# Ten of every sixteen scan units injected by VectorE, Silu as one activation, sums of exp(q) by TensorE, and modulation columns used where they lie

## The chip, the cores and the metric

The kernel runs on one NeuronCore of a Trainium2 chip. The metric is device time in microseconds (us) from the start to the end of one execution. The core has five engines that run side by side and meet at semaphores: TensorE (PE), VectorE (DVE), ScalarE (ACT), GpSimd (POOL) and SyncE (SP, which here only issues DMAs).

## What is computed

x has 8 sequences of 512 tokens with 256 features, float32. Four conditioned layers follow each other; the condition `c` has 512 numbers for each sequence. Layers 0 and 3 are linear attention, layers 1 and 2 are selective scans (Mamba). Cut to what matters:

```python
# layers 0 and 3 (16 and 8 heads; in layer 0 the product's orientation differs)
xn = layernorm(x) * g + b
q  = softmax(xn @ Wq + bq, over the features of a head)
k  = softmax(xn @ Wk + bk + mask, over the tokens)
v  = (xn @ Wv + bv) * mask
y  = q @ (k.T @ v)                       # per head
scale, shift = split(silu(c) @ W_emb + b_emb)
h  = layernorm(y) * (1 + scale) + shift
x  = x + silu(h) @ W_out + b_out
# layers 1 and 2
shift, scale, gate = split(silu(c) @ W_ada + b_ada)
xz = (layernorm(x) * (1 + scale) + shift) @ W_in     # layer 2: tokens permuted
u, z = split(xz);  u = silu(conv4(u))
dt_r, Bm, Cm = split(u @ W_x);  dt = softplus(dt_r @ W_dt + b)
for t in tokens:                          # 512 channels x 16 states
    h = h * exp(dt[t] * A) + (dt[t] * u[t]) * Bm[t];  y[t] = (h * Cm[t]).sum()
x = x + gate * ((y + u * D) * silu(z)) @ W_out
```

## The kernel before

**Units.** Each scan (one sequence in one of layers 1 and 2, so 16 scans in all) is cut into 64 units: one of 16 states of one of 4 chunks of 128 channels, a tile of 128 channels by 512 tokens. 1024 units follow each other. Of unit g, ACT makes the decay exp(dt * A) (L887, L903), somebody multiplies dt*u with the row B ("injects"), DVE runs the recurrence as one `tensor_tensor_scan` (L1160, L1163), POOL multiplies the state with the row C (`weight`, L673), and PE adds the result into a bank of y (L1463). Some groups of four tiles are first added to others by a DMA that POOL issues (L677).

**Two kinds of unit.** `KINDS` says which kind each of 16 consecutive units has. BESIDE: POOL injects from SBUF into the state tile (L664), and ACT writes the decay into one of three PSUM banks (L887). SPREAD: ACT copies the row B into the PSUM bank (`b_row_in_bank`, L895) and writes the decay to SBUF (L903), and DVE injects in the bank (L1153). The bank for unit g+2 is filled while unit g is due, and ACT may fill it only when the scan of unit g-1 has ended (`past(act, m_scan, g - BANKS + 1)`). POOL injects unit g+3 and weights unit g-2.

**Everything else is woven in.** Beside the units run chains of work, each a Python generator per engine: 16 attentions (`attention`: layernorm, turns, k, q, v, the mixing product `mix`, y, a second layernorm, the activation `hid`, the output), 16 preparations (`before`: norm, in-projection, convolution, step sizes), 16 ends of scans (`after`: gate row, gated output weights, output, in layer 2 the permuting back), and at the very start the set-up (`setup`: products of silu(c) with the conditioning weights `c0` to `c3`, L1202; modulation columns `m0` to `m3`; gate rows). For each kind of chain a table (`ATT_STAGES`, `PREP_STAGES`, `POST_STAGES`, `TAIL_STAGES`, `SETUP_STAGES`) gives the number of steps each stage lasts; `timeline` stretches the chain over a range of units, and `run_batches` writes each engine's instructions in that order. Every engine then works in that fixed order and waits where a semaphore isn't there yet. The names of the stages are also the places in the tables.

**What the change touches.** The attention's activation is made from tanh, which stands with exp in one activation table: ACT writes s*h into SBUF (L796) and tanh(s*h) into the bank (L797), DVE joins them (L1086). The modulation columns of a sequence are copied by POOL from `mod_all` to `mod_att` and `mod_prep` (L618, L640), and `gate_pick` (L654) picks one row of the gates, with which ACT makes `gate_row` (L871) for a PE product that spreads it over the partitions (L1426). DVE sums exp(q) over each head (L1068) and takes the reciprocal (L1069) ahead of the mixing. An ACT_TABLE_LOAD stands in ACT's order wherever the next function isn't in the table that is loaded: silu, softplus and exp are in three different ones.

Of the kernel before, what the change touches and what calls it, by code (L numbers as in the profile page):

```python
# [5 lines left out]
P = 128  # L6
# [17 lines left out]
SLOTS = 4  # L24
# [39 lines left out]
MOD_PICK = 8 * DC + 2 * TT  # L64
MODS = MOD_PICK + 1
# [14 lines left out]
def by_name(names, durations):  # L80
# [4 lines left out]
    "first": (3, 19, 20, 20, 31, 13, 4, 6, 28, 4, 62, 1, 1, 2, 9, 13, 10, 15, 0, 2, 11, 15, 37, 4, 14, 6, 0, 2, 30,  # L85
              16, 10, 1, 18, 17, 29, 26, 34, 15, 65, 18, 9, 1, 11, 0, 10, 3, 12, 0, 20, 7, 4, 14),
    "second": (2, 1, 3, 2, 0, 4, 0, 3, 3, 4, 4, 2, 3, 3, 3, 0, 0, 4, 0, 2, 5, 14, 1, 22, 2, 0, 16, 3, 1, 0, 2, 0, 6,
# [9 lines left out]
    "last": (8, 7, 10, 2, 26, 4, 13, 17, 8, 24, 13, 58, 8, 11, 1, 12, 8, 4, 27, 33, 3, 6, 46, 2, 11, 1, 34, 2, 16, 11,  # L97
             12, 12, 5, 20, 5, 6, 6, 5, 60, 0, 20, 8, 12, 15, 5, 6, 22, 17, 4, 1, 3, 4),
})
PREP_STAGES = by_name(PREP_NAMES, {  # L100
    "first": (5, 9, 3, 1, 2, 3, 0, 4, 5, 3, 0, 4, 7, 4, 0, 1, 4, 5, 9, 1, 6, 9, 4, 9),
# [4 lines left out]
})  # L106
POST_STAGES = by_name(POST_NAMES, {
# [4 lines left out]
})  # L112
TAIL_STAGES = by_name(TAIL_NAMES, {
    0: (3, 14, 7),
    1: (0, 32, 4),
    2: (14, 7, 5),
    3: (34, 17, 9),
})
SETUP_STAGES = dict(zip(SETUP_NAMES, (0, 1, 1, 0, 15, 38, 1, 22, 3, 24, 3, 10), strict=True))
# [209 lines left out]
def bass_cond_seq(nc, x, out, mask_cols, keep_cols, mask_rows0, mask_rows3, order, const_pack, att_packs, ssm_packs,  # L329
# [4 lines left out]
    with ctx:  # L334
# [29 lines left out]
        def cw(name):  # L364
# [4 lines left out]
        ones_row8 = cw("ones")[on_gates, :]  # L369
# [11 lines left out]
        mod_att = sb("mod_att", [P, 2 * DC + TT])  # L381
        mod_prep = sb("mod_prep", [P, 2 * DC])
        gate_pick = sb("gate_pick", [P, 1])
# [14 lines left out]
        gate_row = sb("gate_row", [P, D])[on_gates, :]  # L398
# [65 lines left out]
        o_pick, o_row = sem("gate_picked"), sem("gate_row")  # L464

        def past(eng, sem_, count):

# [1088 lines left out]
```

## Time and profile before

| | |
|---|---|
| median of 3 runs | 2323.63 us (2316.66 to 2324.0) |
| profiled execution | 2320.92 us; its span 2318.9 us |
| before the first unit (to about 137 us) | set-up, first preparation, first attention |
| the units (about 137 to 2235 us) | 2098 us for 1024 units |
| behind them | end of the last scan, the last two attentions |
| POOL busy | 2000.3 us (86%) |
| DVE busy | 1980.6 us (85%) |
| PE busy | 1931.7 us (83%) |
| ACT busy | 1691.9 us (73%) |
| granted TensorE clock, mean | 0.928 |

The profile was taken of one execution. Busy is a union of spans: one instruction may begin a little before the one ahead of it has ended, so the distance from start to start is somewhat below a mean duration. "idle before" a group, and who released it, tell what an engine waited for.

### The profile page before, as it was taken

To read this page: it belongs to the slowest core of one execution; us is meant where nothing else is said; L and a number is where in the kernel's file an instruction comes from. 1 tells how busy PE (TensorE), PEld (TensorE's weight loads), DVE (VectorE), ACT (ScalarE), POOL (GpSimd) and SP (SyncE) were. 2 spreads that over 40 slices of the span, in tenths; PEclk is the share of its full clock that TensorE was granted. 3 is DMA by queue.
4 is the path that set the end of the run, shared out by engine and by line. 5 is a ranking of instruction groups with operands and counts; after the bars stand their busy time and mean duration, and the time that the engine had idled before them with its cause. 6 is when DMAs were issued, how large, how long until landed. Compare 5 with 4: busy or idle time off the path is not lost. (4 is left out here: it accounts for less than half of the span.)

```text
span 2318.9 us, 23892 instructions
## 1 busy us (share of the span) xinstructions
PE 1931.7 (83%) x5712; PEld 984.9 (42%) x5712; DVE 1980.6 (85%) x2705; ACT 1691.9 (73%) x2677; POOL 2000.3 (86%) x1720
## 2 busy tenths in 40 slices
PE   6767779898888889889888979889898978778786
PEld 5433324445444444435444444435445443333353
DVE  4468888989989898998989898998989998898862
ACT  2476868697787869688787968778796867678642
POOL 0079998989899998999899998998999999999950
PEclk9887989899999999899999999999999999898997
DMA  6046565655455565555546565564556555565620
GB/s 229 1 135 170 157 181 143 181 155 161 145 166 167 153 191 155 164 166 153 159 143 180 160 178 158 159 174 142 160 157 180 163 157 180 161 175 162 173 77 19
DMA packets 170538, 358.84 MB, mean 155 GB/s; under 512 B 19528, under 2 KB 27936, under 8 KB 161696
## 3 DMA queue, kind: packets, MB, share of 16 engines
q1 hardware_dynamic: 151504, 275.38, 36.3%
q0 software_dynamic: 9216, 67.11, 15.5%
q10 hardware_dynamic: 9680, 14.83, 1.8%
q8 instruction: 47, 0.77, 0.1%
q14 instruction: 91, 0.75, 0.1%
HBM read 284.85 MB, written 5.29 MB: 125 GB/s over the span
## 5 line engine op out<-in xcount | busy, mean ns | idle before, releaser
L673 POOL TENSOR_TENSOR state<-state,c_rows 128x512 f32<-128x512 f32 x1024 | 1313.3, 1340 | 86.5 <-DVE state L1160 46.3
L1463 PE MATMUL bank<-state,const_sb 128*128 128x512 f32 x1536 | 766.7, 617 | 84.9 <-POOL state L673 78.8
L1163 DVE TENSOR_TENSOR_SCAN state<-decay,bank 128x512 f32<-128x512 f32 x576 | 687.8, 1203 | 18.9 <-ACT decay L903 17.6
L664 POOL TENSOR_TENSOR state<-kept,b_rows 128x512 f32<-128x512 f32 x448 | 589.5, 1316 | 0.1
L895 ACT ACTIVATE bank<-b_rows 128x512 f32<-128x512 f32 x576 | 342.3, 594 | 294.6 <-DVE state L1160 240.4
L1160 DVE TENSOR_TENSOR_SCAN state<-bank,state 128x512 f32<-128x512 f32 x448 | 544.1, 1215 | 7.8 <-POOL state L664 7.1
L1153 DVE TENSOR_TENSOR bank<-kept,bank 128x512 f32<-128x512 f32 x576 | 392.5, 681 | 113.4 <-ACT bank L895 110.4
L1463 PEld LDWEIGHTS bank<-state,const_sb 128*128 128x128 f32 x1536 | 282.3, 196 | 408.3 <-issue 210.4
L903 ACT ACTIVATE decay<-kept,ssm_pack 128x512 f32<-128x512 f32 x576 | 409.2, 710 | 2.7 <-issue 1.6
L887 ACT ACTIVATE bank<-kept,ssm_pack 128x512 f32<-128x512 f32 x448 | 304.0, 679 | 31.2 <-DVE state L1163 25.6
L1361 PE MATMUL bank<-kept,ssm_pack 128*128 128x512 f32 x512 | 256.7, 637 | 32.2 <-DVE kept L1113 14.5
L1264 PE MATMUL bank<-att_pack,xnT 128*128 128x256 f32 x768 | 246.1, 445 | 0.0
L1361 PEld LDWEIGHTS bank<-kept,ssm_pack 128*128 128x128 f32 x512 | 100.2, 204 | 160.0 <-issue 106.7
L1264 PEld LDWEIGHTS bank<-att_pack,xnT 128*128 128x128 f32 x768 | 144.1, 209 | 45.5 <-issue 13.3
L1417 PE MATMUL bank<-kept 128*128 128x256 f32 x512 | 138.6, 421 | 14.3 <-DVE kept L1128 14.3
L605 POOL TENSOR_TENSOR att_rstd<-att_var_eps,neg_half 128x4 f32<-128x4 f32 x32 | 33.9, 1058 | 127.2 <-DVE att_minus L1020 127.2
L1113 DVE SCALAR_TENSOR_TENSOR kept<-bank,ssm_pack,kept 128x511 f32<-128x511 f32 (+2 forms) x192 | 128.8, 739 | 16.4 <-ACT kept L828 16.3
L1417 PEld LDWEIGHTS bank<-kept 128*128 128x128 f32 x512 | 107.2, 214 | 50.4 <-issue 36.1
L1245 PE MATMUL bank<-const_sb,xn 128*128 128x128 f32 x384 | 63.7, 295 | 69.4 <-ACT xn L727 39.1
L629 POOL TENSOR_TENSOR kept<-kept 128x1024 f32<-128x1024 f32 x32 | 76.4, 2388 | 50.7 <-ACT kept L809 48.6
L1262 PE MATMUL bank<-bias_rows,right_rows 3*128 3x256 bf16 x192 | 56.1, 292 | 55.1 <-ACT kexp L761 20.3
L1245 PEld LDWEIGHTS bank<-const_sb,xn 128*128 128x128 f32 x384 | 46.9, 150 | 119.7 <-ACT xn L727 52.6
(144 smaller groups left out, 2090.3 us busy)
## 6 DMA issues: line engine op xcount, KB each, us to landing
b_rows<-flat_rows SPq DMA_DIRECT2D x512, 256.0 KB, 3.5
c_rows<-flat_rows SPq DMA_DIRECT2D x512, 256.0 KB, 3.3
state<-state POOLq DMA_DIRECT2D x64, 1024.0 KB, 8.3
out<-x_res ACTq DMA_DIRECT2D x8, 512.0 KB, 5.7
x_next<-x ACTq DMA_DIRECT2D x6, 512.0 KB, 4.8
kept<-film_w SPq DMA_DIRECT2D x2, 1024.0 KB, 12.7
ssm_pack<-ssm_pack SPq DMA_DIRECT2D x1, 2035.0 KB, 14.4
ssm_pack<-ssm_pack ACTq DMA_DIRECT2D x1, 2035.0 KB, 22.2
```

Of the source, the lines that this page charges most:

```text
L664: pool.tensor_tensor(state[:, g % STATES], dtu[:, c], b_rows[:, row % ROWS], ALU.mult).then_inc(m_inject[BESIDE], 1)
L673: pool.tensor_tensor(st, st, c_rows[:, row % ROWS], ALU.mult).then_inc(m_prod, 1)
L887: act.activation(mix_banks[g % BANKS][:], dt[:, c, :], ACT.Exp, scale=neg_a[scan_of(si)[0]][:, c * N + n:c * N + n + 1]).then_inc(m_decay[ ...
L895: act.activation(mix_banks[g % BANKS][:], b_rows[:, row % ROWS], ACT.Copy).then_inc(m_brow, 1)
L903: act.activation(decay[:, nth(g) % DECAYS, :], dt[:, c, :], ACT.Exp, scale=neg_a[scan_of(si)[0]][:, c * N + n:c * N + n + 1]).then_inc(m_d ...
L1153: dve.tensor_tensor(row[:], dtu[:, c, :], row[:], ALU.mult).then_inc(m_inject[SPREAD], 1)
L1160: ins = dve.tensor_tensor_scan(st, mixed, st, 0.0, ALU.mult, ALU.add)
L1163: ins = dve.tensor_tensor_scan(st, decay[:, nth(g) % DECAYS], mixed, 0.0, ALU.mult, ALU.add)
L1264: ins = pe.matmul(dst, lhs[:, c, t * P:(t + 1) * P], weights[:, c, :], start=(c == 0 and bias is None), stop=(c == DC - 1))
L1361: ins = pe.matmul(dst[:], w_in[:, c, (at + e) * P:(at + e + 1) * P], xnT_[:, c, :], start=(c == 0), stop=(c == DC - 1))
L1417: ins = pe.matmul(dst[:, (t % 2) * D:(t % 2 + 1) * D], lhs[:, c, t * P:(t + 1) * P], weights[:, c, :], start=(c == 0), stop=(c == CH - 1))
L1463: pe.matmul(y_banks[c2][:], ident, state[:, g % STATES], start=False, stop=(g == in_bank[-1])).then_inc(m_sum, 1)
```

## The change

1. `KINDS` is ((BESIDE, SPREAD) x 3, SPREAD, SPREAD) twice instead of (BESIDE, SPREAD) x 7, SPREAD, SPREAD: of 16 units 10 are SPREAD, before 9. Of 1024 units 64 change their kind.
2. The attention's activation is one Silu on ACT; the tanh, the product on DVE and the factors 0.5 go. The set-up's silu(c) is made the same way.
3. The sums of exp(q) are eight products of the transposed exp(q) with a few columns of the head mask on PE, written beside the mixing product into the same bank; DVE takes the reciprocal straight from there, behind `mix`.
4. Scale, shift and mask columns are read from `mod_all` in place; POOL's three copies go. The spread gate row comes from one product with a broadcast column of the identity; ACT's `gate_row` goes.
5. All tables of stages have new numbers, and two ranges of units: the set-up lasts to -55 instead of -66, the first preparation runs from -80 to -19 instead of -79 to -14.

```diff
-KINDS = (BESIDE, SPREAD) * 7 + (SPREAD, SPREAD)
+KINDS = ((BESIDE, SPREAD) * 3 + (SPREAD, SPREAD)) * 2
-SETUP_UNITS, FIRST_PREP, FIRST_ATT = (-147, -66), (-79, -14), (-71, 34)
+SETUP_UNITS, FIRST_PREP, FIRST_ATT = (-146, -55), (-80, -19), (-71, 34)
...
-SETUP_STAGES = dict(zip(SETUP_NAMES, (0, 1, 1, 0, 15, 38, 1, 22, 3, 24, 3, 10), strict=True))
+SETUP_STAGES = dict(zip(SETUP_NAMES, (2, 0, 10, 8, 24, 36, 3, 14, 0, 29, 7, 30), strict=True))
...
 # POOL, attention / before / after
-                before_attention(pool, ai)
-                pool.wait_ge(s_mod[layer], 1)
-                pool.tensor_copy(mod_att[:], mod_cols(b, MOD_AT[layer], 2 * DC + TT)).then_inc(a_mod, 1)
...
-                    taken(pool, prep_fill(pi - 1, "turn0"))
-                    taken(pool, prep_fill(pi - 1, "turn1"))
-                pool.tensor_copy(mod_prep[:], mod_cols(b, MOD_AT[layer], 2 * DC)).then_inc(p_mod, 1)
...
-                pool.tensor_copy(gate_pick[:], mod_cols(b, MOD_PICK, 1)).then_inc(o_pick, 1)
...
 # ACT, set-up / attention / after
-            act.activation(silu_c[:].rearrange("p k b -> p (k b)"), cw("cond"), ACT.Tanh, scale=0.5).then_inc(s_silu_t, 1)
+            act.activation(silu_c[:].rearrange("p k b -> p (k b)"), cw("cond"), ACT.Silu).then_inc(s_silu, 1)
...
-                act.wait_ge(a_mod, ai + 1)
+                if b == 0:
+                    act.wait_ge(s_mod[layer], 1)
...
-                    act.activation(xnT[:, c, :], pa[:], ACT.Identity, **args)
-                    act.activation(pa[:], pa[:], ACT.Tanh, **args).then_inc(a_hid, 1)
+                    act.activation(xnT[:, c, :], pa[:], ACT.Silu, scale=scale[:, c:c + 1],
+                                   bias=shift[:, c:c + 1]).then_inc(done, 1)
...
-                act.activation(gate_row, gate_nat[:, layer - 1, :], ACT.Copy, scale=gate_pick[on_gates, :]).then_inc(o_row, 1)
...
 # DVE, attention
-                link(dve.tensor_reduce(qstat[:, 0:TT * heads], q[:].rearrange("p t (g w) -> p (t g) w", w=width), AX, ALU.add))
-                link(dve.reciprocal(qstat[:, 0:TT * heads], qstat[:, 0:TT * heads]))
...
                 pa, done = att_filled(dve, ai, "mix")
+                link(dve.reciprocal(qstat[:, 0:TT * heads], pa[:, DC * P:DC * P + TT * heads]))
...
-                    dve.scalar_tensor_tensor(xnT[:, c, :], pa[:], 1.0, xnT[:, c, :], ALU.add, ALU.mult).then_inc(done, 1)
...
 # PE, attention / after
+                att_taken(pe, ai, "qT0", "qT1")
+                per_chunk = HEADS[at] // DC
+                for t in range(TT):
+                    for c in range(DC):
+                        first = DC * P + (t * DC + c) * per_chunk
+                        ins = pe.matmul(pa[:, first:first + per_chunk], qT[:, c, t * P:(t + 1) * P],
+                                        aw(layer, "heads")[:, ::P // per_chunk], start=True, stop=True)
                 ins.then_inc(done, 1)
...
-                pe.wait_ge(o_row, qi + 1)
-                pe.matmul(dst[:, 0:D], ones_row8, gate_row, start=True, stop=True).then_inc(done, 1)
+                pe.matmul(dst[:, 0:D], ident[on_gates, GATES_AT + b:GATES_AT + b + 1].broadcast_to([B, P]),
+                          gate_nat[:, layer - 1, :], start=True, stop=True).then_inc(done, 1)
```

**ACT, the activation of one attention in the middle of the program** (stage `hid0` and `hid1`; L895, L903 and L887 are the units' copies and decays, in the changed kernel L875, L883 and L867; L796 with L797 and L779 are the attention's activation). Before:

```order
L895 ACTIVATE bank<-b_rows 128x512
L796 ACTIVATE xnT<-bank,mod_att 128x512
L797 ACTIVATE bank<-bank,mod_att 128x512
L903 ACTIVATE decay<-kept,ssm_pack 128x512
L887 ACTIVATE bank<-kept,ssm_pack 128x512
L895 ACTIVATE bank<-b_rows 128x512
L903 ACTIVATE decay<-kept,ssm_pack 128x512
L887 ACTIVATE bank<-kept,ssm_pack 128x512
L796 ACTIVATE xnT<-bank,mod_att 128x512
L797 ACTIVATE bank<-bank,mod_att 128x512
```

The same place of the changed kernel:

```order
L779 ACT_TABLE_LOAD
L779 ACTIVATE xnT<-bank,mod_all 128x512
L875 ACTIVATE bank<-b_rows 128x512
L883 ACT_TABLE_LOAD
L883 ACTIVATE decay<-kept,ssm_pack 128x512
L867 ACTIVATE bank<-kept,ssm_pack 128x512
L875 ACTIVATE bank<-b_rows 128x512
L883 ACTIVATE decay<-kept,ssm_pack 128x512
L867 ACTIVATE bank<-kept,ssm_pack 128x512
L779 ACT_TABLE_LOAD
L779 ACTIVATE xnT<-bank,mod_all 128x512
```

The tanh is gone, and the table is changed ahead of and behind each Silu. In 10 of the 16 attentions both Silus stand behind one load (22 loads at L779 in all). ACT's whole order has 186 table loads before and 232 in the change.

**PE at the start of the program** (L1202 and L1166 are the conditioning products, `kept` holding the weights of stage `c0` and `state` those of `c1`; L1245 and L1209 turn the first attention's normed input; L1251 and L1215 are its k). Before:

```order
L1202 MATMUL bank<-silu_c,kept 128x8 x16
L1202 MATMUL bank<-silu_c,state 128x8 x16
L1245 MATMUL bank<-const_sb,xn 128x128 x8
L1251 MATMUL bank<-xnT,att_pack 128x512 x2
L1253 MATMUL bank<-right_rows,bias_rows 128x512
```

In the changed kernel:

```order
L1166 MATMUL bank<-silu_c,kept 128x8 x16
L1209 MATMUL bank<-const_sb,xn 128x128 x4
L1166 MATMUL bank<-silu_c,state 128x8 x4
L1209 MATMUL bank<-const_sb,xn 128x128 x4
L1166 MATMUL bank<-silu_c,state 128x8 x12
L1215 MATMUL bank<-xnT,att_pack 128x512 x2
L1217 MATMUL bank<-right_rows,bias_rows 128x512
```

The sixteen products of `c1` moved from ahead of the turns to between and behind them, ahead of the first k. (Each row counts a product once; on the chip a float32 product runs as two instructions.)

**ACT at the start of the program** (L718 and L699 exponentiate A, L720 and L701 make the skip diagonal, L727 and L708 norm the first attention's input). Before:

```order
L746 DMA right_rows<-mask_adds 3x512
L727 ACTIVATE xn<-x_next,att_shift,att_rstd 128x256
L718 ACTIVATE ssm_pack<-ssm_pack 128x64
L720 ACTIVATE skip_diag<-const_sb,ssm_pack 128x128 x4
L727 ACTIVATE xn<-x_next,att_shift,att_rstd 128x256 x3
```

In the changed kernel:

```order
L727 DMA right_rows<-mask_adds 3x512
L699 ACT_TABLE_LOAD
L699 ACTIVATE ssm_pack<-ssm_pack 128x64
L701 ACTIVATE skip_diag<-const_sb,ssm_pack 128x128 x4
L708 ACTIVATE xn<-x_next,att_shift,att_rstd 128x256 x4
```

A table load was added ahead of the norm, behind the wait of the DMA.

## Rows read from the trace of the kernel before

**Rows 1.** The stretch of the units: length, busy us (instructions) by engine, clock, DMA.

```profile
core 0: us, PE busy (x) PEld busy (x) DVE busy (x) ACT busy (x) POOL busy (x), PEclk, DMA share, GB/s
137.00:2235.00 2098.00, 1767.12 (x5045) 876.67 (x5045) 1901.28 (x2505) 1615.58 (x2544) 1984.14 (x1690) 0.93 0.57 163
```

**Rows 2.** Costliest groups, whole run: xcount | busy us, mean ns | idle before, releaser.

```profile
L673 POOL TENSOR_TENSOR state<-state,c_rows 128x512 f32<-128x512 f32 x1024 | 1313.3, 1340 | 86.5 <-DVE state L1160 46.3 <-DVE state L1163 39.4
...
L895 ACT ACTIVATE bank<-b_rows 128x512 f32<-128x512 f32 x576 | 342.3, 594 | 294.6 <-DVE state L1160 240.4 <-DVE state L1163 32.5 <-DVE x_res L1090 12.2
```

**Rows 3.** DVE's waits from 254 to 2130 us: total us, times, longest.

```profile
DVE bank L1153 <- ACT bank L895: 85.3, 83, 2.9
DVE qstat L1063 <- PE bank L1264: 20.1, 15, 4.5
DVE state L1163 <- ACT decay L903: 15.7, 19, 5.9
DVE kept L1174 <- PE bank L1463: 10.0, 8, 2.5
DVE qstat L1068 <- ACT xn L771: 8.2, 6, 1.9
DVE state L1160 <- POOL state L664: 4.7, 8, 0.8
DVE xnT L1086 <- ACT bank L797: 4.0, 5, 1.5
```

**Rows 4.** ACT's waits for POOL from 254 to 2130 us.

```profile
ACT xn L727 <- POOL att_shift L607: 41.5, 21, 3.3
...
ACT kept L727 <- POOL prep_shift L607: 20.5, 7, 5.5
ACT gate_row L871 <- POOL gate_pick L654: 12.9, 15, 2.1
```

**Rows 5.** Timeline of POOL, and of DVE, near 700 us: start, length, instruction.

```profile
699.57 1.27 POOL L664 TENSOR_TENSOR state<-kept,b_rows 128x512 f32<-128x512 f32 x1
700.79 2.50 POOL L673 TENSOR_TENSOR state<-state,c_rows 128x512 f32<-128x512 f32 x2
...
701.47 0.66 DVE L1086 SCALAR_TENSOR_TENSOR xnT<-bank,xnT 128x512 f32<-128x512 f32 x1
702.05 0.68 DVE L1153 TENSOR_TENSOR bank<-kept,bank 128x512 f32<-128x512 f32 x1
702.65 1.22 DVE L1160 TENSOR_TENSOR_SCAN state<-bank,state 128x512 f32<-128x512 f32 x1
```

**Rows 6.** Groups that the change removes, whole run, as in rows 2.

```profile
L797 ACT ACTIVATE bank<-bank,mod_att 128x512 f32<-128x512 f32 x32 | 23.8, 742 | 0.0
...
L1068 DVE TENSOR_REDUCE qstat<-xn 128x64 f32<-128x1024 f32 (+1 forms) x16 | 19.3, 1208 | 10.4 <-ACT xn L771 10.4
...
L618 POOL COPY mod_att<-mod_all 128x8 f32<-128x8 f32 x16 | 4.2, 262 | 10.5 <-DVEq L985 10.5
```

**Rows 7.** Table loads: the largest group, and the timeline of ACT around one.

```profile
L903 ACT ACT_TABLE_LOAD x62 | 79.5, 1283 | 1.1
...
668.05 0.60 ACT L895 ACTIVATE bank<-b_rows 128x512 f32<-128x512 f32 x1
668.67 1.28 ACT L903 ACT_TABLE_LOAD   x1
669.96 0.72 ACT L903 ACTIVATE decay<-kept,ssm_pack 128x512 f32<-128x512 f32 x1
```

**Rows 8.** Timeline of PE in the first 60 us.

```profile
20.22 7.00 PE L1202 MATMUL bank<-silu_c,state 128*128 128x8 f32 x32 [0.25 <-DMA state<-ada_w]
30.35 1.97 PE L1245 MATMUL bank<-const_sb,xn 128*128 128x128 f32 x8 [3.14 <-ACT xn L727]
33.28 3.68 PE L1251 MATMUL bank<-xnT,att_pack 128*128 128x512 f32 x4 [0.96 <-ACT xnT L755]
...
53.43 3.64 PE L1202 MATMUL bank<-silu_c,kept 128*128 128x8 f32 x32
```

**Rows 9.** Timeline of PE in the last attention, between activation and output.

```profile
2306.34 0.37 PE L1262 MATMUL bank<-bias_rows,right_rows 3*128 3x256 bf16 x1 [2.77 <-issue]
```

More of the change, by code:

```diff
@@ L63 @@
 MOD_AT = {0: 0, 3: 2 * DC + TT, 1: 4 * DC + 2 * TT, 2: 6 * DC + 2 * TT}
-MOD_PICK = 8 * DC + 2 * TT
-MODS = MOD_PICK + 1
+MODS = 8 * DC + 2 * TT
 GATES_AT = 64
@@ L614, in attention @@
                 root(att_norm, a_var, a_rlink, a_rstd, 2 * ai + 1)
-                yield from w.to("v0")
-                before_attention(pool, ai)
-                pool.wait_ge(s_mod[layer], 1)
-                pool.tensor_copy(mod_att[:], mod_cols(b, MOD_AT[layer], 2 * DC + TT)).then_inc(a_mod, 1)
                 yield from w.to("yroot")
@@ L651, in after @@
             def after(qi, layer, s, b):
-                stages = POST_STAGES[qi % SLOTS]
-                w = Walk(stages)
-                pool.tensor_copy(gate_pick[:], mod_cols(b, MOD_PICK, 1)).then_inc(o_pick, 1)
-                yield from w.to("end")
+                yield from Walk(POST_STAGES[qi % SLOTS]).to("end")
             def inject(g):
@@ L778, in attention @@
                         ins = act.activation(v[:, t, :], pa[:, (t % 2) * D:(t % 2 + 1) * D], ACT.Copy,
-                                             scale=mod_att[:, 2 * DC + t:2 * DC + t + 1])
+                                             scale=keep[:, t:t + 1])
                     ins.then_inc(done, 1)
@@ L793, in attention @@
                     yield from w.to(f"hid{c}")
[L794 to L797 removed]
+                    pa, done = att_filled(act, ai, f"yT{c}")
+                    act.activation(xnT[:, c, :], pa[:], ACT.Silu, scale=scale[:, c:c + 1],
+                                   bias=shift[:, c:c + 1]).then_inc(done, 1)
                 yield from w.to("done")
@@ L818, in before @@
                 yield from w.to("xT")
-                act.wait_ge(p_mod, pi + 1)
+                scale, shift = mod_cols(b, MOD_AT[layer], DC), mod_cols(b, MOD_AT[layer] + DC, DC)
+                if b == 0:
+                    act.wait_ge(s_mod[layer], 1)
                 for c in range(DC):
                     bank_, done = filled(act, prep_fill(pi, f"turn{c}"))
-                    act.activation(prep_xnT[s][:, c, :], bank_[:], ACT.Identity, scale=mod_prep[:, c:c + 1],
-                                   bias=mod_prep[:, DC + c:DC + c + 1]).then_inc(done, 1)
+                    act.activation(prep_xnT[s][:, c, :], bank_[:], ACT.Identity, scale=scale[:, c:c + 1],
+                                   bias=shift[:, c:c + 1]).then_inc(done, 1)
                 for first in (0, 2):
@@ L866, in after @@
                 w = Walk(stages)
-                if qi > 0:
-                    taken(act, post_fill(qi - 1, "gate"))
-                act.wait_ge(s_gate_nat, 2)
-                act.wait_ge(o_pick, qi + 1)
-                act.activation(gate_row, gate_nat[:, layer - 1, :], ACT.Copy, scale=gate_pick[on_gates, :]).then_inc(o_row, 1)
                 if layer == 2:
@@ L940, in _ @@
             dve.wait_ge(s_const, 16)
-            dve.wait_ge(s_silu_t, 1)
-            flat_c = silu_c[:].rearrange("p k b -> p (k b)")
-            setup_link(dve.scalar_tensor_tensor(flat_c, flat_c, 1.0, cw("cond"), ALU.add, ALU.mult))
-            dve.tensor_scalar(flat_c, flat_c, 0.5, None, ALU.mult).then_inc(s_silu, 1)
             keep0, keep3 = (mod_all[:, :, MOD_AT[n] + 2 * DC:MOD_AT[n] + 2 * DC + TT] for n in ATT)
@@ L981, in modulation @@
                     setup_link(dve.tensor_tensor(to_h, to_h, sh, ALU.add))
-                if is_att:
-                    both = mod_all[:, :, MOD_AT[layer]:MOD_AT[layer] + 2 * DC]
-                    setup_link(dve.tensor_scalar(both, both, 0.5, None, ALU.mult))
                 dve.sem_inc(s_mod[layer], 1)
@@ L1081, in attention @@
                 moments(att_norm, y, a_var, link)
-                for c in range(DC):
-                    yield from w.to(f"act{c}")
-                    dve.wait_ge(a_hid, ai * DC + c + 1)
-                    pa, done = att_bank(ai, f"yT{c}")
-                    dve.scalar_tensor_tensor(xnT[:, c, :], pa[:], 1.0, xnT[:, c, :], ALU.add, ALU.mult).then_inc(done, 1)
                 for h in range(2):
```

53 lines of the change are left out of this document (21 added, 32 removed), and 34 rows, old and new, of tables (ATT_STAGES, POST_STAGES, PREP_STAGES).

## The prediction

> **What bounds the kernel now.** I read the stretches first, then who waits for whom, then the timelines. The units take 2098 of 2319 us. In them POOL is busy for 1984 us and idle for 114, DVE is busy for 1901 and idle for 197, PE is busy for 1767 and ACT for 1616 [rows 1]. By busy time alone POOL is the bound. The waits say something else. POOL, the busiest, waits for DVE's scans for 86.5 us [rows 2], while DVE waits for POOL's injections for 4.7 us in 1876 [rows 3]. What DVE waits for is ACT: 85.3 us for the copied B row and 15.7 for a decay, then PE (20.1 and 10.0) [rows 3]. ACT in turn waits for DVE to free a bank, 240.4 and 32.5 us over the run [rows 2], and for small results of POOL that stand in POOL's order behind weightings, 41.5, 20.5 and 12.9 us [rows 4]. So it is a ring of three engines with two to five units between them, and DVE, not POOL, sets its pace most of the time; POOL's load reaches DVE mostly by way of ACT and PE.
>
> **The change part by part.** The sum is made against the profiled execution, 2320.9 us (its span 2318.9 and 2.0 around it), which lies 0.1% under the median.
>
> *POOL's work.* 64 injections go. From start to start one takes 1.22 us [rows 5], so 64 x 1.22 = 78 us; the copies, of which `mod_att` is the largest group with 4.2 us [rows 6], are at most 3 x 4.2 = 12.6, say 10. POOL loses 88 of 1984 us and falls to 1896.
>
> *DVE's work.* 64 injections come: 702.65 - 702.05 = 0.60 us each, 38 us. The join of tanh goes: 32 x (702.05 - 701.47) = 32 x 0.58 = 19 us [rows 5]. The sum over exp(q) goes, 19.3 us [rows 6]. The reciprocal stays. 38 - 19 - 19 = 0: DVE keeps its 1901 us and becomes the busiest engine by 5 us.
>
> *Waits that go with the removed instructions.* DVE waits 8.2 us for exp(q) ahead of the sum and 4.0 for tanh [rows 3]; over the whole stretch times 2098/1876, 14 us. Not all need vanish, since the next instruction could wait instead, but what came next was there in the cases I looked at: **-14 us**, bounds -14 and 0.
>
> *What POOL's relief gives DVE.* Nothing is one bound. The other: POOL was the limit throughout, the most loaded engine keeps the idle time that POOL has now, and the stretch becomes 1901 + 114 = 2015 us, 83 less. Between them I count the waits that hang on POOL [rows 3, 4]: 4.7 directly, 10.0 for the last sums of a chunk (PE waits for weightings there), 20.1 for q (PE comes to it through sums that wait for POOL), and of the 74.9 us in which ACT waits for POOL a third, 25, because ACT runs two units ahead and the rest is hidden. That is 60, times 2098/1876 = 67 us. POOL's lateness doesn't disappear; it shrinks by 4% of its work, and the small results still wait for DVE's statistics. I take somewhat over half: **-39 us**, bounds 0 and -83.
>
> *ACT's work.* 64 more copies of 0.594 us [rows 2] are 38 us. Gone are 32 tanh, 23.8 us [rows 6], about 0.17 us at each of 32 remaining activations (a Silu in place of an Identity with two column operands), 5, and 16 gate rows of about 0.5, 8: together 37. These cancel. What is left is 46 more table loads at 1.283 us [rows 7], 59 us: ACT goes from 1616 to 1675 of about 2070, 81%. Its cover is ACT's idle time, which is largest where DVE is busy with attention work. How much of a load reaches DVE? If all that DVE waited for ACT in rows 3 (101 us in 1876, so 113 in the stretch) is put to the 186 loads, a load costs 0.61 us; that is too much, since some waits stand behind late results of POOL. I take 0.5: **+23 us**. Bounds: 0 (all loads fall into idle time), and 46 x 1.283 = 59. What the cover is worth can be read beside the other loads: a Softplus or Silu of the preparation stands between two loads, and the decay and the copy of the next units stand behind both.
>
> The Trainium skill (ScalarE: Activation LUTs, "What ACT_TABLE_LOAD costs") gives a switch of tables 1283 ns for the load and about 1380 ns for a drain ahead of it, 2.66 us in all. The load agrees to the digit; the drain isn't seen here, since the load begins 0.02 us after the copy before it has ended and the decay 0.01 us after the load [rows 7]. By the page 46 switches would be 122 us of ACT instead of 59, and at the same share my term would be 48 instead of 23.
>
> *PE's work.* Eight products of at most 8 columns in an attention are 16 instructions. The nearest row has 32 instructions of that size in 3.64 us [rows 8], 0.114 each: 1.8 us an attention, 29 us in all. PE is idle for 331 us of the stretch [rows 1], and the mixing bank is waited for little: 0, bounds 0 and +15. The spread gate row no longer waits for POOL and ACT; PE gains that, and no one waits for it long: 0.
>
> *The start, ahead of the units.* Two things come on a chain that nothing hides: the first attention, whose output the first preparation needs. First, ACT's load ahead of the norm, 1.28 us, behind the mask DMA's wait. Second, the 16 products of `c1`, 7.00 us at this place [rows 8], ran while PE waited for the norm; now they stand behind it and ahead of k. Turns from 31.6: 2.0 us of turns and 7.0 of products put k at 40.6 instead of 33.28 [rows 8], +7.3. Later in the same attention the sums add 1.8 us and the reciprocal stands ahead of the mask product, but 32 products of `c2` fill PE just there in both kernels; and the activation gets shorter by about 2 us, since it ends with the Silu and its table can be loaded while PE turns. Together **+7 us**, bounds +2 (the chain has slack where PE wasn't needed at once) and +12.
>
> *The end.* The last attention has 1.8 us of sums and 0.35 of a reciprocal more, and PE's 2.77 us of waiting for the activation [rows 9] shrinks by about 2: **0**, bounds -3 and +3.
>
> *New numbers in the tables.* They move nearly every instruction by some places. I can't price that from rows; the order shows no stage on a wrong side of a unit it needs except in the set-up. 0, and it widens the range by 15 us on both sides.
>
> Sum: 2320.9 - 14 - 39 + 23 + 7 + 0 = 2297.9, rounded **2298 us**, 1.1% below the median.
>
> **The rivals.**
>
> *POOL was the limit.* For it: POOL is busy 94.6% of the stretch, DVE 90.6% [rows 1]. If DVE's waits for ACT only take the place of waits for POOL that would otherwise come, relief of POOL counts fully: 2320.9 - 83 - 14 + 7 + 13 (half the loads' price) = 2244. Against it: POOL waits for DVE over ten times as long as DVE for POOL.
>
> *The gains and the loads cancel.* POOL's relief is worth a fifth, since the ring waits at DVE in any case: 2320.9 - 14 - 15 + 23 + 7 = 2322. For it: the same waits.
>
> *ACT becomes the bound in bursts; slower than before.* At `hid` a pair of loads in the middle of the units' decays (see ACT's order) takes 2.57 us from an engine that is two units ahead. A pair of units with one copy more needs ACT for 2 x 0.71 + 2 x 0.59 = 2.6 us where both are SPREAD, DVE for about 3.5, so ACT catches up by only 0.9 us in such a pair. Where a pair of loads comes within about three units behind another pair, the lead is used up and each further load reaches DVE whole: 46 x 1.283 = 59, and POOL's relief then gives nothing, as DVE is late for another reason: 2320.9 - 14 + 59 + 7 = 2373. It decides from the point where a load costs DVE over 0.9 us in the mean and the relief is under 30 us: 2320.9 - 14 - 29 + 42 + 7 = 2327. The middle of this case is 2345.
>
> **How the numbers follow.** About 0.3% (7 us) is what a measurement of this kernel can tell from no change, so 2317 to 2331 is "the same". Forecast: 0.45, its own range 2278 to 2316. POOL was the limit: 0.17 (2235 to 2278). Cancelled: 0.17 (2316 to 2331). Slower by bursts: 0.21 (2327 to 2375). The range 2258 to 2342 leaves out about half of the first rival and half of the last, 0.19. Faster: 0.45 + 0.17 and a little of the cancelled case, 0.64; same 0.16; slower 0.20.
>
> **What would show it.** POOL busy for about 1910 us over the run and 1896 in the units, DVE within 10 us of 1981, and ACT at about 1750 with 232 loads. DVE's waits for L1117 from ACT (the copy) up by about 15 us rather than by 50; the waits of DVE for q and of ACT for `att_shift` down by a third or more. The first scan starts 7 us later, at about 144 us. Wrong: if DVE's total idle time in the units is unchanged or higher with POOL idle for 200 us, the relief was worth nothing and DVE had the pace alone; if DVE's idle time falls to about 115, POOL had been the limit. If the first k starts at 33 us, the start's term is wrong.

## The result, and the profile after

| | median us (range, runs) | to the kernel before, 95% interval |
|---|---|---|
| before | 2323.82 (2316.66 to 2325.74, 4) | |
| changed | 2341.94 (2341.45 to 2342.7, 4) | 1.0084 [1.0062, 1.0105] |

The change makes the kernel 0.8% slower; 2298 us and a gain were forecast. The page of the changed kernel, with the busy time of each engine and two rows of the busy tenths in 40 slices of the span:

```profile
span 2339.6 us, 24238 instructions
...
PE 1977.6 (85%) x5968; PEld 1048.0 (45%) x5968; DVE 1978.8 (85%) x2716; ACT 1758.4 (75%) x2739; POOL 1919.4 (82%) x1608
...
PE   6776779899888989889898989889898888777796
...
POOL 0059998988798898988898898898889899999950
```

And the stretch of the units, with the columns of [rows 1]:

```profile
141.00:2255.00 2114.00, 1807.96 (x5262) 934.56 (x5262) 1908.98 (x2530) 1682.21 (x2611) 1903.60 (x1582) 0.91 0.56 162
```

The busy times moved much as forecast: POOL's fell from 1984 to 1904 us, DVE's stayed (1901 to 1909), ACT's rose by 67 for 59 forecast, and PE's rose by 41 for 29 forecast. Yet the stretch got 16 us longer, so POOL is now idle for 210 us and DVE for 205 (before 114 and 197): POOL's relief didn't shorten DVE's idle time. Where DVE waits, from 254 to 2130 us, as in [rows 3]:

```profile
DVE bank L1117 <- ACT bank L875: 96.6, 88, 4.8
DVE qstat L1040 <- PE bank L1275: 21.8, 9, 5.0
DVE state L1127 <- ACT decay L883: 12.7, 32, 2.0
DVE x_next L1054 <- PE bank L1228: 10.3, 6, 2.6
DVE kept L1138 <- PE bank L1434: 9.9, 12, 1.5
DVE qstat L1035 <- PE bank L1228: 9.2, 6, 2.8
DVE x_res L1099 <- PE bank L1388: 7.3, 5, 3.4
```

The wait for the copied row rose by 11 us, the wait for q halved. New is the second line: the reciprocal, ahead of the mask product, waits for the sums on PE. A wait of ACT for POOL is all but gone; of the same stretch, to be held against [rows 4]:

```profile
ACT kept L708 <- POOL prep_shift L600: 1.0, 1, 1.0
ACT xn L708 <- POOL att_shift L600: 0.4, 2, 0.2
```

The timelines of PE and DVE at one mixing of the changed kernel (start, length, instruction, idle time before it):

```profile
956.75 3.76 PE L1268 MATMUL bank<-xnT,v 128*128 128x128 f32 x16 [0.78 <-ACT kexp L772]
960.29 1.91 PE L1275 MATMUL bank<-att_pack,kexp 128*128 128x8 f32 x16
...
956.39 2.32 DVE L1127 TENSOR_TENSOR_SCAN state<-decay,bank 128x512 f32<-128x512 f32 x2
962.25 0.56 DVE L1040 RECIPROCAL qstat<-bank 128x64 f32<-128x64 f32 x1 [3.53 <-PE bank L1275]
962.84 0.42 DVE L1041 TENSOR_TENSOR att<-bank,att_pack 128x256 f32<-128x256 f32 x1
```

DVE has nothing to do from 958.7 to 962.3, while PE makes the second half of the mixing products and then the 16 sums. The next scan stands behind this in DVE's order.

### The profile page after: what moved, and what is told of

The parts are those of the page before. It is cut to its first block and busy times, and to the rows that moved or that the text cites. A ratio compares the mean times of both kernels' runs of the same rounds, so it can differ in the third digit from the quotient of the medians.

```text
span 2339.6 us, 24238 instructions
## 1 busy us (share of the span) xinstructions
PE 1977.6 (85%) x5968; PEld 1048.0 (45%) x5968; DVE 1978.8 (85%) x2716; ACT 1758.4 (75%) x2739; POOL 1919.4 (82%) x1608
## 5 line engine op out<-in xcount | busy, mean ns | idle before, releaser
L1127 DVE TENSOR_TENSOR_SCAN state<-decay,bank 128x512 f32<-128x512 f32 x640 | 763.0, 1205 | 16.1 <-ACT decay L883 14.7
L875 ACT ACTIVATE bank<-b_rows 128x512 f32<-128x512 f32 x640 | 380.1, 594 | 285.1 <-DVE state L1124 210.9
L1117 DVE TENSOR_TENSOR bank<-kept,bank 128x512 f32<-128x512 f32 x640 | 435.7, 681 | 121.3 <-ACT bank L875 119.8
L645 POOL TENSOR_TENSOR state<-kept,b_rows 128x512 f32<-128x512 f32 x384 | 512.1, 1334 | 0.1
L1124 DVE TENSOR_TENSOR_SCAN state<-bank,state 128x512 f32<-128x512 f32 x384 | 466.2, 1214 | 3.8 <-POOL state L645 3.4
L883 ACT ACTIVATE decay<-kept,ssm_pack 128x512 f32<-128x512 f32 x640 | 454.7, 710 | 4.3 <-ACT x_dbl L822 1.9
L1434 PEld LDWEIGHTS bank<-state,const_sb 128*128 128x128 f32 x1536 | 290.8, 197 | 349.6 <-issue 218.1
L867 ACT ACTIVATE bank<-kept,ssm_pack 128x512 f32<-128x512 f32 x384 | 261.0, 680 | 76.4 <-DVE state L1127 65.5
L1388 PE MATMUL bank<-kept 128*128 128x256 f32 x512 | 149.3, 443 | 28.3 <-DVE kept L1092 28.2
L1388 PEld LDWEIGHTS bank<-kept 128*128 128x128 f32 x512 | 114.6, 229 | 68.8 <-issue 51.8
L1209 PE MATMUL bank<-const_sb,xn 128*128 128x128 f32 x384 | 66.0, 303 | 59.2 <-ACT xn L708 31.4
```

Source lines behind the costliest of these rows:

```text
L645: pool.tensor_tensor(state[:, g % STATES], dtu[:, c], b_rows[:, row % ROWS], ALU.mult).then_inc(m_inject[BESIDE], 1)
L867: act.activation(mix_banks[g % BANKS][:], dt[:, c, :], ACT.Exp, scale=neg_a[scan_of(si)[0]][:, c * N + n:c * N + n + 1]).then_inc(m_decay[ ...
L875: act.activation(mix_banks[g % BANKS][:], b_rows[:, row % ROWS], ACT.Copy).then_inc(m_brow, 1)
L883: act.activation(decay[:, nth(g) % DECAYS, :], dt[:, c, :], ACT.Exp, scale=neg_a[scan_of(si)[0]][:, c * N + n:c * N + n + 1]).then_inc(m_d ...
L1117: dve.tensor_tensor(row[:], dtu[:, c, :], row[:], ALU.mult).then_inc(m_inject[SPREAD], 1)
L1124: ins = dve.tensor_tensor_scan(st, mixed, st, 0.0, ALU.mult, ALU.add)
```

## The experiments

Each part is either undone in the changed kernel or done alone in the kernel before. The runs were made in four jobs; the median of the kernel before was 2320.3, 2324.5, 2320.9 and 2321.5 us in them, so differences between kernels of different jobs carry about 4 us. Ratios are to the kernel before in the same job. Where a difference is between jobs, it is given from the medians, and behind it, where it matters, from the ratios.

### Which part of the change loses

**Kinds as before (9 of 16 by DVE).**

```diff
-KINDS = ((BESIDE, SPREAD) * 3 + (SPREAD, SPREAD)) * 2
+KINDS = (BESIDE, SPREAD) * 7 + (SPREAD, SPREAD)
```

> The changed kernel (2342 us) with the kinds of units of before: 9 of 16 SPREAD instead of 10; all else as changed. Theory P (VectorE has the pace, so 64 injections moved to it cost their 38 us and GpSimd's relief gives little back): 2342 - 38 + 10 = about 2314, with GpSimd's idle time in the units back from 210 to about 120 us. Theory R (the move is worth what I forecast, and the loss comes from the Silus, the sums and the tables): slower than the changed kernel, about 2370. If within 7 us of 2342, moving injections is neutral.

2341.38 us, ratio 1.0082 [1.006, 1.0104]: no difference to the changed kernel, though POOL is busy for 75 us more (1994.5) and DVE for 35 us less (1943.4 instead of 1978.8). So in the changed kernel the trade is worth nothing: POOL's relief gives back what the injections cost on DVE, no more. Theory P expected 2314 from DVE's 38 us, so DVE doesn't have the pace alone either.

**Tanh as before.**

```diff
-                    act.activation(xnT[:, c, :], pa[:], ACT.Silu, scale=scale[:, c:c + 1],
-                                   bias=shift[:, c:c + 1]).then_inc(done, 1)
+                    act.activation(xnT[:, c, :], pa[:], ACT.Identity, **args)
+                    act.activation(pa[:], pa[:], ACT.Tanh, **args).then_inc(a_hid, 1)
```

> The changed kernel with the attention's activation made by tanh again (Identity and Tanh on ScalarE, the join on VectorE, the factor 0.5), all else as changed. Theory L (the 46 added table loads cost VectorE 0.5 to 1.3 us each): 2342 - 23 to 59, plus 19 us for the joins on VectorE: 2302 to 2338. Theory P says VectorE's 19 us of joins weigh most: 2350 to 2360. 186 table loads or a few more by either.

2362.9 us, 1.019 [1.0168, 1.0212]: Silu gains 21 us (25 by the ratios), its table loads included. DVE's wait for the join (15.6 us from 254 to 2130 us) is back with its work, 4.0 in the kernel before [rows 3].

**Sums of exp(q) on DVE as before.**

```diff
-                link(dve.reciprocal(qstat[:, 0:TT * heads], pa[:, DC * P:DC * P + TT * heads]))
+                yield from w.to("v0")
+                att_taken(dve, ai, "q0", "q1")
+                link(dve.tensor_reduce(qstat[:, 0:TT * heads], q[:].rearrange("p t (g w) -> p (t g) w", w=width), AX, ALU.add))
+                link(dve.reciprocal(qstat[:, 0:TT * heads], qstat[:, 0:TT * heads]))
...
-                att_taken(pe, ai, "qT0", "qT1")
...
...
-                    att_taken(pe, ai, "mix")
+                    att_taken(pe, ai, "qT0", "qT1", "mix")
```

> The changed kernel with the sums of exp(q) on VectorE again. Theory S (the reciprocal behind the mixing product makes VectorE wait for TensorE: 24 us in the units after the change, 47.6 over the run, against 8 for the sum and 1 for the mask product before): 2342 - 24 - 5 (TensorE's own time at both ends) + 19 (the sums on VectorE) + 5 = about 2337. Theory P: 2342 + 19 = 2361.

**2303.3 us**, 0.9933 [0.9913, 0.9952]: 38.6 us faster than the changed kernel (35 by the ratios) and 0.7% faster than the kernel before, although DVE has 17 us more to do. It beats both, and I call it D from here on. Taking this one part out removes the whole loss. The same mixing in D:

```profile
936.60 2.32 DVE L1130 TENSOR_TENSOR_SCAN state<-decay,bank 128x512 f32<-128x512 f32 x2
940.47 0.42 DVE L1044 TENSOR_TENSOR att<-bank,att_pack 128x256 f32<-128x256 f32 x1 [1.55 <-PE bank L1271]
```

From the end of the scan to the end of the mask product it is 1.97 us here, and 4.55 in the changed kernel (from 958.71 to 963.26). Over all 16 attentions these pieces sum to 61.9 us in the changed kernel and 23.5 in D, 38.4 more. That this is the 38.6 us lost is partly chance: D makes the sums and the reciprocals elsewhere on DVE (19.3 and 7.2 us), so about 27 us of the loss lie at other places.

**Old tables and ranges.**

```diff
-SETUP_UNITS, FIRST_PREP, FIRST_ATT = (-146, -55), (-80, -19), (-71, 34)
+SETUP_UNITS, FIRST_PREP, FIRST_ATT = (-147, -66), (-79, -14), (-71, 34)
...
```

> The changed kernel with all stage tables and unit ranges of before. If the new numbers are what loses (theory T): 2342 - 16 or more = under 2326, and the first k back at 33 us. If they were neutral: 2342 - 5 for the start = 2337. If they fit the changed kernel better than the old ones: over 2350.

2397.14 us, 1.0329 [1.0308, 1.035]: the new tables are worth 55 us to the new code. ACT's waits for POOL are back although POOL has the light load (of the stretch of [rows 4]):

```profile
ACT xn L708 <- POOL att_shift L600: 39.0, 21, 3.3
ACT kept L708 <- POOL prep_shift L600: 18.3, 4, 5.7
```

With the new tables and the old kinds the first of them is 2.3 us. So it is mainly the new tables that take these waits away, not the relief of POOL; the second wait is 7.9 us there, so the relief has a part in that one.

**POOL's relief without the sums on PE** (D with the old `KINDS`).

> The changed kernel with the sums on VectorE again (e3, 2303 us) and also 9 of 16 units SPREAD. With the sums on TensorE the kinds made no difference (2341 and 2342). Theory P (VectorE has the pace): VectorE loses 38 us of work, so 2303 - 28 = 2275. Theory N (both engines hold each other; what one loses the other's waits take up): 2303 within 7. Theory R (relief of GpSimd was worth having once the wait for the sums is gone): 2315 to 2330.

2318.59 us, 0.998 [0.997, 0.999]. Against D, 15.3 us (11 by the ratios): once the sums are away, the trade gains, although it costs DVE 33 us of work.

### Why the sums on PE cost so much

**Idle sums.** D, with the products of the sums added on PE behind the mixing products, ahead of their signal; nobody reads them.

```diff
                                         across[:, t, c * P:(c + 1) * P], start=(t == 0), stop=(t == TT - 1))
+                att_taken(pe, ai, "qT0", "qT1")
+                per_chunk = HEADS[at] // DC
+                for t in range(TT):
...
+                        ins = pe.matmul(pa[:, first:first + per_chunk], qT[:, c, t * P:(t + 1) * P],
+                                        aw(layer, "heads")[:, ::P // per_chunk], start=True, stop=True)
                 ins.then_inc(done, 1)
```

> Kernel e3 (sums on VectorE, 2303 us), and TensorE computes the 128 x 2 small products as well, ahead of the signal that the mixing product is ready; nobody reads them. This adds TensorE's time, its wait for the transposed exp(q) and the later signal, without the reciprocal behind it and with VectorE's sum still there. If these make the loss (theory S1): 2303 + 35 to 60 = about 2345 or more (the sum on VectorE is still paid). If VectorE's order is what costs (theory S2, the reciprocal in the chain): under 2315.

2344.3 us, 1.0087 [1.0073, 1.0101]. This is 41.0 us over D (36 by the ratios). The whole loss is back, with DVE's old sums and reciprocal in their place: it is PE's side.

**The reciprocal late.** D, with only the reciprocal moved behind the wait for the mixing product.

> Kernel e3 (2303 us) with the reciprocal alone moved behind the wait for the mixing product, where the changed kernel has it; the sums stay on VectorE where they were. Theory S1: within 7 us of 2303. Theory S2: 2320 or more.

2318.43 us, 0.9975 [0.9965, 0.9985]: 15 us over D (10 by the ratios) for 16 instructions of 0.44 us. It lies between the two theories. The idle sums didn't have this, and still cost 41. If the three simply added up, with the 19.3 us of the sum that goes [rows 6] counted in full, the changed kernel would have 41 + 15 - 19.3 = 37 us, or 27 by the ratios, beside the 38.6 or 35 measured. The price of the sum on DVE wasn't measured alone, so this is no proof that they add up.

**The mask product later in the order.** The changed kernel with the stage `mix` four steps longer in all attentions but the first and the last, later stages four steps shorter.

> The changed kernel (2342 us) with the stage in which VectorE takes the reciprocal and the mask product four steps later (some two units) for all attentions beside units but the first and last; the later stages are squeezed by four steps. If VectorE simply comes to the sums too early for the time that TensorE needs (theory S3, a matter of the tables): VectorE's wait there falls from 24 to under 8 us and the time by 10 to 20 us, to 2322 to 2332. If the wait moves to y and the norm behind: 2342 or more.

2397.45 us, 1.0317 [1.0303, 1.0331]. The wait for the sums fell to 2.2 us, as expected, but DVE waited 41.1 us for y instead of 2.5 (both from 254 to 2130 us), and the time rose by 55. The wait was moved on rather than removed. (The sums with a signal of their own, behind that of the mixing products, were not tried: DVE would read a bank while PE writes it.)

**The wait alone.** D, with PE's wait for the transposed exp(q) ahead of the last mixing product, and no further product.

```diff
                     for t in range(TT):
+                        if c == DC - 1 and t == TT - 1:
+                            att_taken(pe, ai, "qT0", "qT1")
```

> The changed kernel with the sums of exp(q) back on VectorE (2303 us), in which TensorE additionally waits for both copies of the transposed exp(q) ahead of the last of its eight mixing products; no further product is made. This is one half of what the idle sums added (2344 us), the wait without the 16 small products. Theory W (it is the wait: the mixing bank is signalled only once ScalarE has copied qT1, and VectorE, in order, stands at the mask product): most of the 41 us, 2330 to 2345. Theory P (it is the time that the 16 products take on TensorE in front of the signal, about 1.8 us an attention at 0.11 us each, 16 times): within 5 us of the kernel without them, 2298 to 2309. A value near 2320 shares it out. If W, VectorE's waits at the mask product are about 24 us as with the idle sums; if P, under 8.

2303.54 us, 0.9923 [0.991, 0.9935]: nothing. DVE's wait at the mask product over the whole run is 17.8 us, as in D, where the idle sums have 42.0.

**Half the products.** The idle sums with `range(TT // 2)`.

> The same kernel with sums on VectorE (2303 us), with the wait for qT and only half of the idle sums behind the mixing products (8 of the 16 small products of an attention, tokens of the first two blocks alone; nobody reads them). Theory P (TensorE's time in front of the signal): half of the 41 us, about 2323. Theory W (the wait): nearly all, 2337 to 2345, since half the products change only 0.9 us of each chain.

2323.5 us, 1.0008 [0.9996, 1.0019]: 20.0 us over the kernel with the wait alone in the same job, about half the loss of the full products.

**The same products elsewhere.** D, with the idle products in front of the attention's first transpose, in 15 of 16 attentions.

```diff
                     yield from w.to(f"turn{c}")
+                    if c == 0 and ai > 0:
+                        pa, _ = free("turn0")
...
                     pe.wait_ge(a_xn, 2 * ai + 1)
```

> The changed kernel with the sums on VectorE (2303 us), with the same 16 small products that nobody reads, but in front of the attention's first transpose (turn0) and ahead of its wait for the normalised tokens, in 15 of 16 attentions; the mixing signal stays as early as without them. Theory C (the 41 us are the place, since VectorE stands in order behind the mixing signal): little, 2303 to 2313. Theory T (TensorE is the engine with no slack in these stages, and its 27 us of products cost the same wherever they stand): 15/16 of 41 us, 2338 to 2345. Between 2315 and 2333 both have a part.

2332.12 us, 1.0042 [1.0028, 1.0055]: 28.8 us over D (25 by the ratios). So the place explains only a part; most of the cost comes at this second place too. The groups of the products in the three kernels (half, full, elsewhere), whole run:

```profile
L1278 PE MATMUL bank<-att_pack,kexp 128*128 128x8 f32 (+1 forms) x128 | 17.2, 259 | 0.0
```

```profile
L1278 PE MATMUL bank<-att_pack,kexp 128*128 128x8 f32 (+1 forms) x256 | 34.7, 270 | 0.0
```

```profile
L1246 PE MATMUL bank<-att_pack,kexp 128*128 128x4 f32 (+1 forms) x240 | 28.2, 251 | 0.9 <-DVE x_res L1057 0.9
```

| kernel | PE's time in them | cost over D by medians (by ratios) | cost / time |
|---|---|---|---|
| half, ahead of the mixing signal | 17.2 | 20.2 (17) | 1.17 (1.0) |
| full, ahead of the mixing signal | 34.7 | 41.0 (36) | 1.18 (1.0) |
| elsewhere | 28.2 | 28.8 (25) | 1.02 (0.9) |

In these three kernels one us of the products costs about one us of program. Not all of it need be the products' own time. In the kernel with the full idle sums PE is busy for 1984.8 us against 1927.1 in D, 57.7 more, of which the products are 34.7: PE's other work took 23 us longer, at a mean granted clock of 0.905 against 0.920. How much of the 41 us comes by way of that clock, no run separates. Elsewhere a part shows as PE's lateness with the units' last sums: DVE's wait for them, for the whole run, was 11.7 us in D and is now

```profile
L1141 DVE TENSOR_TENSOR kept<-bank,kept 128x512 f32<-128x512 f32 x64 | 43.2, 675 | 22.2 <-PE bank L1438 21.9
```

How can an engine that is idle for 306 us of the changed kernel's stretch be in the way? A slice of 10 us of the kernel before (columns as in [rows 1]):

```profile
770.00:780.00 10.00, 10.00 (x30) 4.79 (x29) 7.09 (x8) 9.91 (x15) 9.74 (x9) 1.00 0.50 130
```

There PE is busy for 10.00 of 10 us and DVE for 7.09. Cut into slices of 10 us from 140 to 2220, the kernel before has 71 of 208 in which PE is busy for 9.5 us or more, and in 23 of them DVE is under 9.0. The changed kernel has 83 of 210 and 40. In such a slice a further product finds no idle time. But these counts don't explain the price at the mixing. In the 10 us about each of the 16 mask products (from 8 ahead of its start to 2 behind) PE is busy for 9.5 us or more in only 2 attentions of the kernel before and 5 of D, and for 7.7 and 8.1 us on average. That full slices of PE are the cause is argued, not shown.

What was short at the mixing was the slack of the one bank, the time from the end of the mixing products to the start of the mask product on DVE. One mixing of the kernel before:

```profile
939.43 2.02 PE L1304 MATMUL bank<-xnT,v 128*128 128x128 f32 x16
...
942.42 0.41 DVE L1072 TENSOR_TENSOR att<-bank,att_pack 128x256 f32<-128x256 f32 x1
```

The products end at 941.45, so DVE comes 0.97 us later and doesn't wait; 16 further products of 1.85 us in all would end behind it. In 8 of the 14 attentions between the first and the last this slack is under 1 us, in 3 it is 2.0 and in 3 about 5. In D it is under 0.25 us in 10 of the 14. The pieces from the instruction ahead of the mask product to its end sum to 48.4 us in the kernel with idle sums against 23.5 in D: 25 of its 41 us are DVE's delay at this place.

### The parts alone on the kernel before

**The sums on PE alone.**

> The kernel before with one part of the change alone: the sums of exp(q) by TensorE beside the mixing product, the reciprocal behind it, no other edit, old tables. If the loss belongs to the part and not to the new tables, this is slower than the kernel before by something like the 38 us that the part costs in the changed kernel: 2340 to 2370. If the loss is one of the new tables alone (they put the mask product at 0 to 6 units behind the mixing product), this lands within 10 us of the kernel before, 2313 to 2333.

2350.79 us, 1.0129 [1.011, 1.0149]: 30 us slower. The loss doesn't hang on the new tables.

**The new tables alone.**

> The kernel before with the new tables of stages and the new ranges alone, no other edit. The old tables cost the changed kernel 55 us. If the new tables are better by themselves, this is faster than the kernel before, 2270 to 2310. If they are only fitted to the changed instructions (kinds of units, activation, sums), they fit the old ones worse: 2330 to 2380, as the old ones do the new code. My forecast in the prediction, that a table is worth at most 15 us either way, would need 2306 to 2337.

2378.22 us, 1.0239 [1.0224, 1.0255]: 57 us slower. The tables are fitted, not better: with the old code ACT waits 33.9 us for `gate_pick` and 24.5 for `mod_att` (from 254 to 2130 us; 12.9 for `gate_pick` with the old tables [rows 4]), small copies of POOL that the change takes out.

**The columns and rows in place alone.**

> The kernel before with the modulation columns and gate rows used in place alone: POOL's three small copies and ScalarE's gate row go, old tables and everything else as before. In the prediction these instructions and the waits for them were worth 14 us together with the join of the activation. If ScalarE's waits for POOL (about 20 us of VectorE's waits lay behind them) are what stood in the path: 2305 to 2317. If another wait takes their place: within 5 us of the kernel before.

2317.54 us, 0.998 [0.9971, 0.9989]: a gain of 4.0 us. ACT's waits for POOL's shifts stayed (41.3 and 19.9 us), only `gate_pick`'s 12.9 went.

**The set-up earlier.** D with `neg` and `c1` 8 to 10 steps earlier.

```diff
-SETUP_STAGES = dict(zip(SETUP_NAMES, (2, 0, 10, 8, 24, 36, 3, 14, 0, 29, 7, 30), strict=True))
+SETUP_STAGES = dict(zip(SETUP_NAMES, (2, 0, 2, 0, 40, 36, 3, 14, 0, 29, 7, 30), strict=True))
```

> The changed kernel with the sums on VectorE (2303 us) and, in the set-up's table, the products c1 eight steps and its neighbours ten steps earlier with the freed steps put in front of the next stage; the later stages of the set-up stand where they did. The start of the changed kernel is 4.9 us later than the one of before, and the 32 products c1 lie in front of the first k in TensorE's order with 6.8 us. If those products are the delay, the first injection comes 3 to 5 us earlier (near 136) and the time is 2298 to 2301. If the start waits for something else (the arrival of the weights), the first injection stays near 140 and the time at 2303.

2306.38 us, 0.9928 [0.9916, 0.9941]: no gain on D (2.8 us over the kernel with the wait alone in the same job), and the first injection came at 145.5 instead of 140.2 in the profiled executions. What sets the start of the units stays open.

## Why the prediction was wrong

**The step that failed** is *PE's work*: "PE is idle for 331 us of the stretch [rows 1], and the mixing bank is waited for little: 0, bounds 0 and +15". The size of the work was nearly right (29 us; 34.4 measured). Its price was not: the same products, read by nobody, cost 41 us in D (36 by the ratios), against 0 and a bound of 15. With 41 in this term the sum is 2338.9 and the sign is right. That it then lies so near the measured 2341.9 is partly luck, since other terms were off in both directions, as the same sum sorted by the parts of the change shows:

| part | forecast by the terms | measured in the changed kernel | measured elsewhere |
|---|---|---|---|
| kinds of units (relief -39, injections on DVE +38) | -1 | 0 | -15 in D |
| sums on PE (sum on DVE -19, its wait -9, PE's work 0) | -28 | +39 | +30 alone |
| Silu (join -19, its wait -5, table loads +23) | -1 | -21 | |
| columns and rows in place | 0 | | -4 alone |
| new tables | 0 (15 either way) | -55 | +57 alone |
| start | +7 | +5 | |

Two things in the step were wrong.

First, the cover. I hid the work behind idle time summed over 2098 us, in a text that says itself that waits, not sums, set the pace. That idle time was no cover: put in front of the attention's first transpose, away from the mixing signal, 28 us of products still cost 25 to 29. The rule of the Trainium skill on this (Perfetto Trace Analysis, "Identifying the Most-Contended Engine") is to judge TensorE's headroom by the share of its weight loads and by flops rather than by busy matmul time. Here weight loads are at 44% in D, which by that rule leaves headroom; the runs disagree, since those products cost nearly their own length. Why PE's idle time can't take them stays open.

Second, the chain. The sums stand between the mixing products and the signal for which DVE stands in order, and the scans stand behind it. I named the reciprocal ahead of the mask product for the first and the last attention (0.35 us at the end) and didn't price it in the 14 between: it alone costs 15 us in D (10 by the ratios). That DVE waited little for the mixing product in the middle of the program (0.8 us from 254 to 2130 us, too little to be among [rows 3]) I took for slack. It was none: in 8 of those 14 attentions DVE came less than 1 us behind the mixing products, and I put 1.8 us between.

**The other terms.** *POOL's relief, -39*: with the 38 us of injections on DVE, which I had netted in *DVE's work*, it came out as forecast beside the sums on PE, and 15 us better without them. The mechanism was partly wrong. I took ACT's waits for POOL's small results as a sign of POOL's load; with the new tables the largest goes at the same load (39.0 to 0.4 us), and with the old kinds it stays away (2.3). *Waits that go, -14*: not measured apart; columns and rows in place gave 4 alone. *ACT's work*: the Silu takes as long as the Identity before (777 and 770 ns on average), not 0.17 us less as I had it, so ACT lost 5 us less work than I counted. *Table loads, +23*: the count was right, 232, and so was ACT's busy time (1758 for about 1750); DVE's wait for the copy rose by 11 us for 15 forecast. Their price wasn't measured apart from the joins that go; together they gained 21. *Start, +7*: the first injection came at 141.3 instead of 136.4, +4.9; k began at 36.48 and not at 40.6, because the norm came earlier (PE's first turn at 28.14 instead of 30.35) and 8 of the 32 instructions of `c1` filled the gap between the turns:

```profile
28.14 1.11 PE L1209 MATMUL bank<-const_sb,xn 128*128 128x128 f32 x4 [9.76 <-ACT xn L708]
29.05 1.71 PE L1166 MATMUL bank<-silu_c,state 128*128 128x8 f32 x8
30.62 1.09 PE L1209 MATMUL bank<-const_sb,xn 128*128 128x128 f32 x4
31.50 5.13 PE L1166 MATMUL bank<-silu_c,state 128*128 128x8 f32 x24
36.48 3.76 PE L1215 MATMUL bank<-xnT,att_pack 128*128 128x512 f32 x4
```

*End, 0*: 89.0 us from the last injection to the end before, 90.0 after. *Tables, 0 with 15 either way*: far too narrow. They are worth 55 us to the new code and cost 57 on the old. A range of 15 for them was no bound from any row.

**The rivals.** The slower case lay at 2345, near the result, but for another reason: bursts of table loads at the activation. Its condition was a load that costs DVE over 0.9 us; the wait for the copy rose by 11 us for 46 loads, 0.24 each, and taking the Silu with its loads out made the kernel slower. POOL as the limit is out as well: POOL idles for 210 us.

**What stays open.** The parts don't add up. From the kernel before to D the kinds give 15, the Silu 21 and the columns in place 4, 40 together, where D is 17 us faster (2303.3 to 2320.3 in the same job). Some 23 us are lost between them, with the start's 4 or 5 among them. I can't say where; each part was measured beside a different rest, and a table fits only one of them. Open too are the 16 of the 41 us of the idle sums that don't lie at the mask product, and the part of the clock in them.

## What to carry to other kernels

Idle time summed over a long stretch is no cover: on an engine busy for 84% of the run, added products cost 0.9 to 1.2 times their own length at both places tried. A wait of nearly zero is no slack either. Before work is put ahead of a signal, read in the timelines how long the signal has been there when the waiting engine comes (here 0.03 to 5.1 us), take off what is added, on both engines, and count what is left over at each occurrence. And when an order is tuned by tables, measure an edit with its own tables and with the old, since here the fit was worth 55 us, more than any single edit.

## What the runs showed of the hardware

The price of a narrow fp32 product. The 16 instructions of the sums (128x8 or 128x4 results) took 1.85 us at a granted clock of 1.00 (the mean from 554.5 to 558.3 us), 0.116 each, hardly less than the 16 mixing instructions of 128 columns just ahead of them, 1.95 us (the third and fourth row below). Here fewer columns bought next to nothing.

And they can fall into TensorE's lower clock. Four timeline rows of PE, the mixing and the sums in two attentions of the changed kernel, and the slice with the granted clock (third number from the end) at the first:

```profile
412.99 3.76 PE L1268 MATMUL bank<-xnT,v 128*128 128x128 f32 x16 [0.78 <-ACT kexp L772]
416.54 3.42 PE L1275 MATMUL bank<-att_pack,kexp 128*128 128x8 f32 x16
...
554.58 1.95 PE L1268 MATMUL bank<-xnT,v 128*128 128x128 f32 x16
556.36 1.85 PE L1275 MATMUL bank<-att_pack,kexp 128*128 128x8 f32 x16
```

```profile
416.00:420.00 4.00, 3.96 (x20) 3.86 (x19) 0.01 (x1) 0.00 (x0) 4.00 (x5) 0.50 0.41 141
```

From 416 to 420 us the granted clock is 0.50, the level of 1.2 GHz, PE having waited three times for ACT just ahead (3.2 us of the ten from 404 to 414, in which it was busy for 6.86), and the same 16 products take 3.42 us instead of 1.85. This happens in 3 of the 16 attentions of the changed kernel. DVE is busy for 0.01 of these 4 us. With the idle sums it is again 3 of 16, and so PE's time for 256 instructions ahead of the mixing signal is 34.7 us, 0.136 each, against 28.2 for 240 in front of the turns, 0.118 each.
